# One mixing product in three fp32r passes, one table buffer, other load queues and orders, in a two-layer adaLN and FFN kernel

## The reference, cut to what matters

```
x1 = x + sum over experts e of gate_e * (gelu(t @ W1_e + b1_e) @ W2_e + b2_e)
```

```
xh = layernorm(x1)
h  = layernorm(xh * pw_g + pw_b) * cp_g ;  t = xh * tm_g ;  s = xh * ms_g
z  = x1 @ Wx + t @ Wt + s @ Ws + h @ Wh + (terms of the states and of the tables' shifts)
y  = layernorm(silu(z) @ int_W2 + int_b2) * int_g + int_be
out = x1 + FFN(y)      # two products in, h1, h2, w3
```

## Time and profile before

| what | us |
|---|---|
| median of 3 runs (lowest, highest) | 433.73 (433.21, 434.11) |
| the profiled execution's own time | 432.91 |
| its span in the trace | 431.1 |
| granted clock of TensorE, mean | 0.994 of full |
| PE busy | 413.5 |
| DVE busy | 312.8 |
| ACT busy | 292.0 |
| POOL busy | 115.0 |

### The profile page before, as it was taken

How to read it: one execution, slowest core, us unless ns; L and a number is a source line. 1 busy time by engine, 2 the same in 40 slices (tenths; PEclk the granted TensorE clock), 3 DMA queues, 4 the chain that set the end, 5 groups by cost and what they waited for, 6 DMA issues and landing times.

```text
span 431.1 us, 5758 instructions
## 1 busy us (share of the span) xinstructions
PE 413.5 (96%) x1812; PEld 270.2 (63%) x1812; DVE 312.8 (73%) x656; ACT 292.0 (68%) x518; POOL 115.0 (27%) x122
## 2 busy tenths in 40 slices
PE   8698899999999999999999999999999999898996
PEld 5475455544656765776567665776577556677774
DVE  5489999987995587658866657678864788666653
ACT  4378967877756874677746884686668474857654
POOL 0026401443426520244153000448035031110000
PEclk9999999999999999999999999999999999999999
DMA  7976637563453342324531160325502210000000
GB/s 235 361 326 175 191 102 190 131 177 98 134 122 106 105 127 65 105 52 119 150 92 38 49 172 2 87 62 172 164 0 65 73 56 0 2 0 26 0 24 27
DMA packets 30216, 45.07 MB, mean 105 GB/s; under 512 B 3717, under 2 KB 22634, under 8 KB 29674
## 3 DMA queue, kind: packets, MB, share of 16 engines
q1 hardware_dynamic: 25504, 32.82, 26.4%
q0 software_dynamic: 3584, 10.49, 7.5%
q10 hardware_dynamic: 1098, 1.40, 1.1%
HBM read 40.68 MB, written 4.03 MB: 104 GB/s over the span
## 4 chain that ended last, share of the span: by engine, by line
PE 78%; DVE 9%; DMA 4%; issue 4%; ACT 3%; ACTq 1%; POOL 1%; SPq 1%; DVEq 0%
PE bank L750 21%; PE bank L648 20%; PE bank L786 7%; PE bank L696 7%; PE bank L640 6%; PE bank L735 5%; PE bank L664 2%; PE bank L703 2%; DMA keepP<-keepP_in 2%; DMA t_split<-tsS 2%; PE bank L775 1%; DVE mG L1190 1%; ACT mG L899 1%; PE bank L555 1%; DVE bn L1199 1%
## 5 line engine op out<-in xcount | busy, mean ns | idle before, releaser
L648 PE MATMUL bank<-mG,W 128*128 128x512 f32 x256 | 119.6, 593 | 0.0
L899 ACT ACTIVATE mG<-bank,keepP 128x512 f32<-128x512 f32 x128 | 85.3, 687 | 27.2 <-PE bank L640 17.6
L1464 POOL TENSOR_TENSOR rstd<-ve,mhalf 128x4 f32<-128x4 f32 x24 | 32.8, 1366 | 203.6 <-DVE ve L1205 203.5
L1190 DVE TENSOR_TENSOR mG<-mG,gwbs 128x1024 f32<-128x1024 f32 x64 | 77.3, 1218 | 2.1 <-DMA gwbs<-gate_w 1.3
L648 PEld LDWEIGHTS bank<-mG,W 128*128 128x128 f32 x256 | 47.5, 189 | 38.9 <-issue 35.3
L640 PE MATMUL bank<-ts,A 96*128 96x512 f32 x128 | 62.2, 526 | 1.7 <-ACT mG L899 1.6
L964 ACT ACTIVATE G<-bank,keepP 128x512 f32<-128x512 f32 x48 | 32.2, 692 | 27.9 <-PE bank L750 27.8
L1445 POOL DMA_INDIRECT gp<-pgb_in,ixall x32 | 35.8, 1119 | 26.7 <-issue 9.1
L750 PE MATMUL bank<-hB_h,h2w_h 128*128 128x512 f32 x96 | 39.7, 414 | 0.0
L750 PE MATMUL bank<-hA_h,h1w_h 128*128 128x512 f32 x96 | 38.7, 403 | 0.0
L1448 POOL DMA_INDIRECT gcm<-ctm,ixcm x32 | 35.1, 1098 | 9.8 <-issue 9.4
(11 more groups left out here) (243 smaller groups left out, 782.4 us busy)
## 6 DMA issues: line engine op xcount, KB each, us to landing
gwbs<-gate_w SPq DMA_DIRECT2D x32, 512.0 KB
keep<-xT_in SPq DMA_DIRECT2D x8, 256.0 KB, 6.0
outT<-keep SPq DMA_DIRECT2D x8, 256.0 KB, 2.1
t_split<-tsS SPq DMA_DIRECT2D x7, 192.0 KB
ts<-t_split SPq DMA_DIRECT2D x7, 192.0 KB
W1T<-W1T_in SPq DMA_DIRECT2D x1, 1024.0 KB, 8.7
W<-W2T_in SPq DMA_DIRECT2D x1, 1024.0 KB, 13.6
hs<-h1T_in SPq DMA_DIRECT2D x1, 1024.0 KB, 8.5
```

Of the source, the lines that this page charges most:

```text
L648: mm = pe.matmul(OACC[:, :], W2[:, e * HC + c, :], mG[n % NMG][:, c, :], start=False, stop=(e == E - 1 and c == HC - 1))
L899: act.activation(mG[e % NMG][:, c % HC, :], HM[n % 2][:, :], ACT.Gelu, bias=b1c[:, c:c + 1]).then_inc(m_gelu, 1)
L1190: dve.tensor_tensor(mine, mine, gate.unsqueeze(1).broadcast_to([P, HC, TT, P]), ALU.mult).then_inc(m_q, 1)
L1464: step(pool.tensor_tensor(rstd[:, n, :], ve[:, n, :], mhalf[:, :], ALU.pow))
```

## The change

- `Z`: the product with x1 stays fp32, its weight is now `wx`. The products with turned t, s and h become three fp32r passes each: `wc[0]` by `turned_hi`, `wc[0]` by `turned_lo`, `wc[1]` by `turned_hi`.
- ACT's `tc`, `sc`, `ch` now write the rounded high half; three new DVE steps per block, `tl`, `sl`, `hl` (`turned_low`), read the bank and the high half and write the low half. `Ts`, `Th` and the next `XT` wait for the low half, and so does each group of passes in `Z`. One ACT copy and one DVE step `zl` split the weight once.
- `gp` and `gcm` are one buffer each: a block is gathered after `hc`, `s` and `t` of the block before it have read the tables.
- `earlyP` is loaded by SP ahead of `W1T`; ACT loads `bdec` and `bdec_u` right after `muT`.
- One more unread product (`fi4`), and new orders for all engines. In the last turn DVE's `t` comes ahead of `hg`, and PE's `Tt` comes after four FFN steps of block 5. The orders of the weights' low halves change too.

```diff
-        wmix = sb("wmix", [P, 4, P])
+        wx = sb("wx", [P, P])
+        wc = [sb(f"wc_{p}", [P, 3, P], F32R) for p in "hl"]
...
-        ct, cs_, ch = [sb(f"c{k}", [P, T]) for k in "tsh"]
+        turned_hi = [sb(f"c{k}_h", [P, T], F32R) for k in "tsh"]
...
PE, turn 7, from XT to YT:
-                "... O6 O7 XT -Fr0 =F4 =F5 -Fr1 =F6 =F7 Tt -Fr2 Ts =F8 =F9 Th -Fr3 Z =F10 Y =F11 -Fr4 -Fr5 YT -Fr6 -Fr7 Fp0 =F12 ..."
+                "... O6 O7 -YT XT =F4 =F5 =F6 =F7 Tt -Fr0 =F8 -Fr1 Ts =F9 Th -Fr2 Z -Fr3 =F10 Y =F11 -Fr4 -Fr5 YT -Fr6 -Fr7 Fp0 =F12 ..."
PE, turn 0:
-                "A0 tm0 tm1 gm0 sq0 A1 A2 tm2 tm3 fi0 gx0 fi1 sq1 A3 tm4 tm5 gm1 gm2 fi2 H0 H1 fi3 ..."
+                "A0 tm0 tm1 gm0 tm2 sq0 A1 tm3 A2 fi0 gm1 gx0 A3 fi1 sq1 fi2 H0 H1 tm4 fi3 tm5 H2 tm6 H3 H4 gm2 fi4 ..."
DVE, turns 6 and 7, in part:
-                (6, "... q5 -s ~fo q6 =u0 q7 -hc =u1"), (7, "q0 ~fl0 ~u2 q1 ... -x ~fl3 -st0 =a -s -t -hg ... x =fl3 st0 -ur0 s hg -ur1 t ...")
+                (6, "... q5 -hc =u0 q6 q7 =u1 =fl0 -sl =u2 -hl x ..."), (7, "q0 -st0 =a -t -hg ... x st0 -flo t hg =fl4 =fl6 -ur0 s tl ...")
...
+            load(earlyP[:, :], A["earlyP"], ld_small)
             load(W1T[:, :], A["W1T"], ld_W1T)
...
             def Ts(b):
                 pe.wait_ge(s_ready, b + 1)
-                pe.wait_ge(tr_out[0], b + 1)
+                pe.wait_ge(tr_lo, 3 * b + 1)
...
-                for m, src in enumerate((keep[b % 3], ct, cs_, ch)):
-                    if m:
-                        pe.wait_ge(tr_out[m - 1], b + 1)
-                    mm = pe.matmul(XL[:, :], wmix[:, m, :], src[:, :], start=False, stop=(m == 3))
+                pe.matmul(XL[:, :], wx[:, :], keep[b % 3][:, :], start=False, stop=False)
+                if b == 0:
+                    pe.wait_ge(wc_lo, 1)
+                for m in range(3):
+                    pe.wait_ge(tr_lo, 3 * b + m + 1)
+                    for n, (w_, c) in enumerate(((0, turned_hi), (0, turned_lo), (1, turned_hi))):
+                        mm = pe.matmul(XL[:, :], wc[w_][:, m, :], c[m][:, :], start=False, stop=(m == 2 and n == 2))
...
+            def turned_low(n, b):
+                dve.wait_ge(tr_out, 3 * b + n + 1)
+                if b:
+                    dve.wait_ge(z_mm, b)
...
+                dve.tensor_tensor(turned_lo[n][:, :], XE[:, :], turned_hi[n][:, :].bitcast(F32), ALU.subtract).then_inc(tr_lo, 1)
...
             def tables(b, t):
-                if b >= 2:
-                    pool.wait_ge(h_ready, b - 1)
+                if b:
+                    pool.wait_ge(h_ready, b)
...
+            load(bdec, A["b_dec"][:, 0:KR * D].rearrange("o (i k) -> (o i) k", k=KR), ld_bd)
+            load(bdec_u, A["b_dec"][:, KR * D:KR * (D + 1)].rearrange("o k -> k o"), ld_bd)
             load(wd_u, A["W_dec"][:, KR * D:KR * (D + 1)].unsqueeze(1).broadcast_to([MU, 2, KR]), ld_wu)
-            load(bdec, A["b_dec"][:, 0:KR * D].rearrange("o (i k) -> (o i) k", k=KR), ld_bd)
             load(Vk[:, :], A["V"], ld_v)
             load(keepP[:, :], A["keepP"], ld_v)
-            load(earlyP[:, :], A["earlyP"], ld_small)
...
-            load(bdec_u, A["b_dec"][:, KR * D:KR * (D + 1)].rearrange("o k -> k o"), ld_bd)
```

More of the change, by code:

```diff
@@ L208, in build @@
         nmr = sb("nmr", [P, 3, TT])
-        gp[1] = sb("gp1", [P, TT, 2 * P])
-        gcm[1] = sb("gcm1", [P, TT, 3 * P])
+        turned_lo = [sb(f"c{k}_l", [P, T], F32R) for k in "tsh"]
+        sb("spare", [P, 992])
         fin = [sb(f"fin_{p}", [P, T], F32R) for p in "hl"]
@@ L255, in build @@
         tr_mm = sems("tt_mm", "ss_mm", "hh_mm")
-        tr_out = sems("t_out", "s_out", "h_out")
+        tr_out, tr_lo = sems("turned_hi", "turned_lo")
+        wc_hi, wc_lo = sems("wc_hi", "wc_lo")
         xT_mm, t_ready, s_ready, h_ready, idx_in, oh_ready, z_mm, z_th, act_ready, y_mm, yT_mm, \
@@ L305, in weights_done @@
         def weights_done(eng, *ns):
-            eng.wait_ge(w_lo, max((4, 2, 1, 3)[n] for n in ns))
+            eng.wait_ge(w_lo, max((4, 3, 1, 2)[n] for n in ns))
         def wide(v, n):
@@ L313, in build @@
             "PE": (
[17 rows of a table removed]
[17 rows of a table added]
             ),
             "ACT": (
[19 rows of a table removed]
[3 rows of a table added]
+                    "-nh tch7 -sc"),
[16 rows of a table added]
             ),
             "DVE": (
[14 rows of a table removed]
[15 rows of a table added]
             ),
             "POOL": (
[L370 to L373, removed]
-                (4, "tab0 =rt2 tab1 -rt1 tab2 tab3"),
-                (5, "tab0 -rt0 tab1 tab2 =rt2 -rt1 -rt2 tab3 rt0 rt1"),
-                (6, "tab0 tab1 tab2 tab3"),
-                (7, "tab0 -rt0 -rt1 =rt2 tab1 tab2 -rt2 tab3 rt0 rt1 rt2"),
[8 rows of a table added]
             ),
             "SP": (
[8 rows of a table removed]
[8 rows of a table added]
             ),
@@ L616, in fold @@
                     pe.matmul(XL[:, 0:P], syT[:, n * B:(n + 1) * B], wsc[:, 2 + n, :], start=(n == 0), stop=(n == 2))
-                for n, w_ in enumerate((3, 1, 2)):
-                    mm = pe.matmul(XE[0:NI, 3 * P:4 * P], tbT[:, n, :], wmix[:, w_, :], start=(n == 0), stop=(n == 2))
+                for n, w_ in enumerate((2, 0, 1)):
+                    mm = pe.matmul(XE[0:NI, 3 * P:4 * P], tbT[:, n, :], wcf[:, w_, :], start=(n == 0), stop=(n == 2))
                 mm.then_inc(fold_mm, 1)
@@ L654, in XT @@
                 if b:
-                    pe.wait_ge(tr_out[2], b)
+                    pe.wait_ge(tr_lo, 3 * b)
                 else:
@@ L929, in turned_out @@
                     act.wait_ge(small_src, NSMALL)
-                act.activation(dst[:, :], XE[:, :], ACT.Copy).then_inc(tr_out[n], 1)
+                act.activation(dst[:, :], XE[:, :], ACT.Copy).then_inc(tr_out, 1)
             def zt(b):
@@ L1067, in ws_ @@
                 act.activation(wint[:, :], iW2, ACT.Copy, scale=0.5)
-                for n, dst in enumerate((wmix[:, 3, :], wmix[:, 1, :], wsc[:, 2, :], wsc[:, 3, :], wsc[:, 4, :], wmix[:, 2, :])):
+                for n, dst in enumerate((wcf[:, 2, :], wcf[:, 0, :], wsc[:, 2, :], wsc[:, 3, :], wsc[:, 4, :], wcf[:, 1, :])):
                     ins = act.activation(dst, iW1[:, n, :], ACT.Copy, scale=aw_e[:, n:n + 1])
                 ins.then_inc(wsc_ready, 1)
+                act.wait_ge(wsc_ready, 1)
+                act.activation(flat(wc[0]), flat(wcf), ACT.Copy).then_inc(wc_hi, 1)
             def load(dst, src, s):
@@ L1248, in oh, with zl @@
                 dve.tensor_scalar(oh8, idx8[32:48, :], iota8[32:48, :], None, ALU.is_equal).then_inc(oh_ready, 1)
+            def turned_low(n, b):
+                dve.wait_ge(tr_out, 3 * b + n + 1)
+                if b:
+                    dve.wait_ge(z_mm, b)
+                else:
+                    dve.wait_ge(terms_out, 64)
+                    dve.wait_ge(terms_in, 16 * 6)
+                    dve.wait_ge(b2_lo, 1)
+                dve.tensor_tensor(turned_lo[n][:, :], XE[:, :], turned_hi[n][:, :].bitcast(F32), ALU.subtract).then_inc(tr_lo, 1)
+            def zl():
+                dve.wait_ge(wc_hi, 1)
+                dve.tensor_tensor(flat(wc[1]), flat(wcf), flat(wc[0]).bitcast(F32), ALU.subtract).then_inc(wc_lo, 1)
             def a(b):
@@ L1331, in s_mix @@
                 dve.wait_ge(wsc_ready, 1)
-                step(dve.tensor_tensor(wmix[:, 0, :], wsc[:, 2, :], wsc[:, 3, :], ALU.add))
-                dve.tensor_tensor(wmix[:, 0, :], wmix[:, 0, :], wsc[:, 4, :], ALU.add).then_inc(small_src, 1)
+                step(dve.tensor_tensor(wx[:, :], wsc[:, 2, :], wsc[:, 3, :], ALU.add))
+                dve.tensor_tensor(wx[:, :], wx[:, :], wsc[:, 4, :], ALU.add).then_inc(small_src, 1)
             def s_n():
@@ L1429, in tables @@
             def tables(b, t):
[L1431 to L1435 removed]
+                if b:
+                    pool.wait_ge(h_ready, b)
+                    pool.wait_ge(s_ready, b)
+                    pool.wait_ge(t_ready, b)
+                else:
                     pool.wait_ge(ix_ready, 1)
```

46 lines of the change are left out of this document (19 added, 27 removed), and 125 rows, old and new, of the table ORDER.

## The result

| | before | after |
|---|---|---|
| median of 6 runs each (lowest, highest), us | 433.76 (433.21, 434.11) | 450.02 (448.04, 451.26) |
| ratio (95% interval) | 1 | 1.0376 (1.0358 to 1.0395) |
| profiled execution, its span, us | 432.91, 431.1 | 448.94, 447.1 |
| granted clock, mean | 0.994 | 0.973 |

The account below looks back on a forecast made before the run. PE was taken as the bound, busy 413.5 of 431.1 us. From the profiled 432.9, less 4.1 (Z), 3.0 (loads), 1.2 (Tt), plus 0.4 (unread product), came 425.0, stated as 425.8 against the median; 8-in-10 range 421.5 to 431.0.

Parts of the forecast that it names:

- Elsewhere I count the orders as neutral; bounds -1 and +3.: Engine orders outside the last turn: no net effect, bounds -1 and +3 us.
- Low halves: New DVE subtractions for turned tiles: 16.4 us more DVE work, hidden behind other PE work; 0 taken, upper end 16.4.
- Z's products: Three fp32r passes for each of t, s, h in Z: 0.51 us less per block, 4.1 over eight.
- the Trainium skill's four passes: Z's fp32 products at four passes each would gain 5.5 us; the prediction let the trace's 0.86 per product decide.
- Rival 4: Z's passes wait for their low halves in turn, gain 0: 429.9 us; chance only part of rival 1's and 2's.
- Loads: Prologue: earlier bdec_u load closes PE's 3.88 us hole, gm0 3.7 us earlier; 3.0 us gained, bounds 0 and 4.7.
- Rival 1: Prologue gives nothing, since loads or the gate chain's DVE work end it at the same time: 428.8 us, chance 0.20.
- The last turn's wait of Tt: Last turn: t ahead of hg on DVE and FFN products before Tt remove PE's wait for t, 1.2 us.
- One table buffer: Gathers after the previous block's hc need about 13.6 us of a 17.0 us gap: cost 0, upper bound 20.5.
- Rival 3: Single buffer makes POOL's tables late, stopping DVE and then PE: slower, up to 439.8 us, chance 0.08.
- Rival 2: DVE becomes the bound from 80 to 120 us, filled by low halves: 430.4, up to 434 us, chance 0.12.

Follow-up runs that it names:

- block 3: Runs of the changed kernel's code with old orders: everywhere 441.67 us, with products moved later 440.62; only in turns 0 and 1 437.69, with that seam mended 433.52.
- the mended hybrid: Changed kernel with turns 0 and 1 in the old orders, the seam's ACT and DVE words mended, early loads and tile addresses as before: 433.52 us, 1.0039.

## Why the prediction was wrong, step by step

**The step that failed** is "Elsewhere I count the orders as neutral; bounds -1 and +3." Taking turns 0 and 1 in the old orders removes about 12 of the 16 us (14.6 less the loads and the addresses, block 3). I had followed the last turn's and the steady turns' orders word by word and the prologue's not at all, though SP's queue had visibly been rearranged there and had no slack shown.

**Low halves, taken as 0.** In the steady turns the number held: after 120 us PE waits 0.5 us for a low half. In turn 1 it didn't: the low halves of block 0 have a wait that those of the other blocks haven't, `terms_in`, and `turned_low(0, 0)` is the first to meet it. The diff moved it there from POOL, where before it had delayed only gathers; it now stops DVE for 5.8 us and PE for 3.94. The working looked at the latency of the copy and the subtraction, and never asked what else the first one waits for.

**Z's products, 4.1 us.** Right. Chain after, the answer to the earlier trace rows:

```profile
392.13 2.08 PE bank L704 x9
```

2.08 against the 2.07 of the working, and Z with its neighbours takes 3.56 us where it took 4.05 (block 3). By the Trainium skill's four passes (FP8 and Floating Point Precision, TensorE Precision Notes) it would have been 0.69 less per block, an estimate of the prediction; the measured 0.49 agrees with the row. Rival 4 fell. But 1.9 to 2.9 us of it, as priced in the kernel before, went to the tiles' new address, which the prediction did not look at.

**Loads, 3.0 us.** Measured alone: 0.5 us slower (0.1 faster to 1.1 slower). The hole went and its parts came back, in PE's timeline after, the answer to the earlier trace rows:

```profile
15.06 0.21 PE L839 MATMUL bank<-keepP,Vk 30*128 30x30 f32 x1 [2.77 <-DMA keepP<-keepP_in]
...
17.19 0.40 PE L834 MATMUL bank<-muT,gap 128*30 128x128 f32 x2
...
22.55 1.05 PE L579 MATMUL bank<-G,tT 32*128 32x8 f32 x8 [1.15 <-DVE tT L1157]
```

`keepP` landed at about 15.0, where the issue at 4.49 and 8.0 to landing had made 12.5. I had let it slip by the 0.4 us of one issue only; what slowed its transfer I have not separated. `gm0` came 1.7 us earlier, not 3.7, and behind it the chain met the new orders. The clock was not full either: 0.90 up to 30 us, 0.94 before. Rival 1, with a chance of 0.20, had this step right.

**The last turn's wait of Tt, 1.2 us.** It is gone, as expected; 0.74 us ahead of an FFN product stand in its place, and from XT(7) to the end the changed kernel takes 74.6 us against 73.4; with the address mended it takes 73.7.

**One table buffer, taken as 0.** In the orders of before it costs 2.4 us. The working compared gathers with the gap between last and first use, and said of the roots behind them that they "belong to statistics that come later still". In turn 1 they don't. The gap was tighter than written, too: a gather lands 4.1 to 4.6 us after its issue in the trace after, where the working took a store's 2.1, and from the end of `hc` the gap of the earlier trace rows is 16.4 us, not 17.0. With that landing the working's 11.5 us of gathers make about 16, for 16.4 of gap. Rival 3 had the sign and not the place: nothing waited for rows in the changed kernel.

**Rival 2,** DVE as the bound from 80 to 120, had the right stretch and the wrong reason: DVE was busy 28.3 of 40 us there, 34.9 before. It waited.

**What stays open.** The changed kernel with SP and POOL mended is still 4.5 us over the mended hybrid; that this is the PE, ACT and DVE orders of turns 0 and 1 follows by elimination (the early loads have 0.5 of it), and no single word of them was tried. Why the steady turns, with Z 0.5 us shorter per block and the address mended, give 2.0 us from Z(1) to the end (306.1 against 308.2) rather than the 4.8 of the prediction's terms (3.6 for Z, 1.2 for Tt), was not separated.

## What to carry to other kernels

A queue that is taken in order turns a reordering into a wait for everything behind it: for each word moved, and each semaphore wait moved to another engine, list what stands behind it until the next transfer that somebody needs soon, in the prologue above all, where no work hides it. Ask also what a late block makes late behind it: B(0), 4.7 us late, came back 15 us later as a gate store 4.8 us late. Count a wait of TensorE more than once, since the products behind it can run at the lower clock. And keep tile addresses fixed when a buffer is removed or added, or pad to the same place, before comparing a few tenths of a per cent.
